# Two expert layers of a hybrid kernel: list constants made early, marks laid out without a step, two result banks, an earlier second list, unread transposes

## What is computed

```
x = x + attn_a(layernorm(x))     # differential attention, 16 heads, causal
x = x + ffn(layernorm(x))        # 8 experts, the best 2 of each token
x = x + attn_b(layernorm(x))     # decayed linear attention, 16 heads of 64
x = x + ffn(layernorm(x))        # the same 8 experts again
```

```
scores = softmax(xf @ router_w.T)              # 2048 tokens x 8 experts
topk_scores, topk_ids = top_k(scores, 2)       # weights, divided by their sum
h   = silu(xf @ w_gate[e]) * (xf @ w_up[e])    # 128 -> 512
out = sum over the two experts of  w * (h @ w_down[e])   # 512 -> 128
```

## Time and profile before

| | us |
|---|---|
| runs of the kernel | 1101.81, 1105.71, 1106.21 (median 1105.71) |
| the profiled execution | 1104.58 |
| its span, first to last instruction | 1102.8 |
| busy in the span: PE, DVE, ACT, POOL | 983.6, 771.8, 733.3, 437.2 |
| mean granted clock of TensorE | 0.962 of 2.4 GHz |

### The profile page before, as it was taken

How to read it: one execution, slowest core, us unless ns; L and a number is a source line. 1 busy time by engine, 2 the same in 40 slices (tenths; PEclk the granted TensorE clock), 3 DMA queues, 4 the chain that set the end, 5 groups by cost and what they waited for, 6 DMA issues and landing times. The chain is left out here.

```text
span 1102.8 us, 27337 instructions
## 1 busy us (share of the span) xinstructions
PE 983.6 (89%) x10398; PEld 663.4 (60%) x10398; DVE 771.8 (70%) x1616; ACT 733.3 (66%) x1475; POOL 437.2 (40%) x584
## 2 busy tenths in 40 slices
PE   5889999999999999964899988999999999489994
PEld 3333333333333333554899877787877887379984
DVE  6789999999999997876433435666766767653342
ACT  4658888888888887624366557677786776445652
POOL 3752212222112221134377433555555553237752
PEclk9889999999999999986999999999999999799998
DMA  2234111111111100241114112121122410011232
GB/s 73 83 95 132 41 31 32 37 54 31 31 31 32 35 27 2 87 144 39 44 54 140 59 49 101 40 78 48 71 100 93 154 69 11 27 42 51 57 87 81
DMA packets 42151, 68.68 MB, mean 62 GB/s; under 512 B 10088, under 2 KB 21096, under 8 KB 40104
## 3 DMA queue, kind: packets, MB, share of 16 engines
q1 hardware_dynamic: 34424, 55.12, 15.5%
q0 software_dynamic: 4992, 10.23, 3.3%
q10 hardware_dynamic: 2608, 1.58, 0.5%
HBM read 51.79 MB, written 14.68 MB: 60 GB/s over the span
## 5 line engine op out<-in xcount | busy, mean ns | idle before, releaser
L803 ACT ACTIVATE PB<-S 128x512 f32<-128x512 f32 x576 | 308.0, 597 | 72.4 <-PE S L609 67.5
L915 DVE TENSOR_REDUCE mx<-S 128x2 f32<-128x1024 f32 (+1 forms) x192 | 207.5, 1127 | 8.6 <-PE S L595 8.6
L871 POOL TENSOR_SCALAR_AFFINE_SELECT PB<-PB 128x512 f32<-128x512 f32 x128 | 79.2, 637 | 307.8 <-ACT PB L803 307.7
L644 PE MATMUL PV<-PB,VP 128*32 128x256 f32 (+2 forms) x2432 | 178.8, 381 | 0.0
L1644 DVE TENSOR_TENSOR m_hs<-m_gs,m_UP 128x512 f32<-128x512 f32 x78 | 53.6, 687 | 141.5 <-ACT m_gs L1530 138.5
L609 PE MATMUL S<-W 50*128 50x512 bf16 (+3 forms) x768 | 124.2, 329 | 4.9 <-ACT PB L803 4.2
L1395 POOL DMA_INDIRECT yd_rows<-m_ys,m_target x78 | 76.8, 985 | 89.0 <-DVE m_ys L1651 77.8
L595 PE MATMUL S<-W 48*128 48x512 bf16 (+3 forms) x640 | 94.5, 326 | 13.1 <-DVE mx L911 4.9
L1526 ACT ACTIVATE m_xt<-m_XT 128x128 f32<-128x128 f32 x78 | 21.6, 277 | 110.7 <-PE m_XT L1437 110.7
L1455 PE MATMUL m_YP<-W,m_hs 128*128 x624 | 84.3, 278 | 11.5 <-DVE m_ys L1651 11.5
L644 PEld LDWEIGHTS PV<-PB,VP 128*32 128x32 f32 x2432 | 51.7, 108 | 69.6 <-issue 59.9
(11 more groups left out here) (384 smaller groups left out, 1892.3 us busy)
## 6 DMA issues: line engine op xcount, KB each, us to landing
d_LQ<-l_rows SPq DMA_DIRECT2D x15, 1024.0 KB, 4.9
W<-qk_parts SPq DMA_DIRECT2D x210, 32.0 KB
qk_parts<-OT SPq DMA_DIRECT2D x24, 256.0 KB, 3.0
W<-qk_parts SPq DMA_DIRECT2D x30, 96.0 KB
W<-in_L_ffn_w_gate SPq DMA_DIRECT2D x1, 2048.0 KB, 9.5
W<-in_L_ffn_w_up SPq DMA_DIRECT2D x1, 2048.0 KB, 14.5
xn_rows<-m_XN SPq DMA_DIRECT2D x8, 256.0 KB, 2.2
m_GA<-yd_rows SPq DMA_DIRECT2D x8, 256.0 KB, 4.3
```

Source lines behind the costliest of these rows:

```text
L644: ins = nc.tensor.matmul(PV[32 * u:32 * u + 32, shift + col:shift + end], VP[:, g, kb, u // 2, :], PB[:, slot, col:end], start=(kb == 0 an ...
L803: nc.scalar.activation(PB[:, j % NPB, :], S2[:, j % 3, :], ACT.Exp, scale=SC).then_inc(exp_done, 1)
L871: nc.gpsimd.affine_select(out=tri, in_=tri, compare_op=ALU.is_ge, fill=0.0, base=0, pattern=[[0, U], [1, P]], channel_multiplier=-1).then_ ...
L915: nc.vector.reduce_max(mx[:, g % 2, c, :, heads[0], qb], S1[:, b, :, 0:w], AX.X)\
```

## The change

1. **Constants.** The constants are allocated once for the whole program (`list_constants`) and made by GpSimd in the attention loop, behind the masks of g == 0 (`make_list_constants`). The semaphore `const_r`, its waits and the memset of `iv` go.
2. **Marks.** `marks` has the tile index i ahead of the planes and slots, so that a product reads its moving operand as one run; VectorE writes (and reads again) the marks through views with the tile index innermost, hence with a step of 3 x slots elements. `place_oh` stays.
3. **Result banks.** `YP` has two banks, used in turn; down(s) waits for y_copy(s-2). The result of the second products moves into the bank of the counts `RC`.
4. **Second list.** `positions` and `late_rows` go ahead of the loop; the marks to slots 0 and 1, the products behind down(2), `other_experts` to slot 2, the sums of the list to the end of slot 3, `make_targets` to 4, `weights` to 5. Three small operations move from `first_bounds` to `second_bounds`. The sums of the list are a copy of the new slots and one addition, in place of three additions.
5. **Unread transposes.** Twenty transposes of the identity stand on TensorE between the first products and the first slot.
6. In `decay_attention` the table `rem` takes the place of `mz`, which is no longer needed by then.

```diff
 def list_products(nc, IV, place_oh, marks, k, start, stop):
-    slots = marks.shape[3]
+    slots = marks.shape[4]
     for i in range(8):
-        last = nc.tensor.matmul(IV[:, 0:planes * slots].rearrange("p (a s) -> p a s", a=planes), place_oh[:, k, :, i],
-                                marks[:, k, 0:planes, :, i], start=(start and i == 0), stop=(stop and i == 7))
+        last = nc.tensor.matmul(IV[:, 0:planes * slots], place_oh[:, k, :, i],
+                                marks[:, k, i, 0:planes].rearrange("p a s -> p (a s)"), start=(start and i == 0),
+                                stop=(stop and i == 7))
...
 def mark_places(nc, chain, tmp, marks, place_oh, slot_no, lane_no, tile_no, iop, k, placed):
-    chain.link(nc.vector.tensor_tensor(marks[:, k, 2], slot_no, ...
-    nc.vector.tensor_tensor(marks[:, k, 0], marks[:, k, 2], ...
-    nc.vector.tensor_scalar(marks[:, k, 1], marks[:, k, 2], ...
+    where, lane, tile = (marks[:, k, :, a].rearrange("p i s -> p s i") for a in (2, 1, 0))
+    chain.link(nc.vector.tensor_tensor(where, slot_no, tmp["slotb"][:, k].unsqueeze(1).to_broadcast(shape), ALU.is_equal))
+    nc.vector.tensor_tensor(tile, where, tile_no.unsqueeze(1).to_broadcast(shape), ALU.mult)
+    nc.vector.tensor_scalar(lane, where, iop, None, ALU.mult)
...
@@ diff_attention, GpSimd, at the end of g == 0
+                            make_list_constants(nc, const)
...
+def make_list_constants(nc, const):
+    nc.gpsimd.memset(const["ones_f"][:], 1.0)
+    nc.gpsimd.memset(const["parts"][:], 0.0)
+    count(const["edges"][:, 0:NT // 2], [[P, NT // 2]], P - 1, 0)
+    count(const["edges"][:, NT // 2:], [[P, NT]], 0, 0)
+    count(const["slot_no"][:], [[1, SLOTS], [0, 8]], 0, 0)
+    count(const["tile_no"][:], [[1, NT]], 1, 0)
+    count(const["iop"][:], [[0, 1]], 0, 1)
+    count(const["lane_no"][:], [[1, P], [0, 8]], 0, 0)
+    count(const["ios"][:], [[1, SLOTS]], 0, 0)
+    count(const["spare"][:], [[P, SLOTS]], 2 * NT * P + 1, 1)
...
@@ moe
-        XT, YP, RC, IV = (ps(k, [P, 512]) for k in ("XT", "YP", "RC", "IV"))
+        XT, RC = (ps(k, [P, 512]) for k in ("XT", "RC"))
+        YP = ps("YP", [P, 2, 512])
...
                 products(IVA, place_a, marks_a, 0)
+                for _ in range(20):
+                    nc.tensor.transpose(GP[:, 1, 0:P], ident[:], ident[:])
                 pe.wait_ge(experts_loaded, loads)
...
                 def down(s, e):
                     pe.wait_ge(h_ready, s + 1)
-                    if s:
-                        pe.wait_ge(y_copied, s)
+                    if s >= 2:
+                        pe.wait_ge(y_copied, s - 1)
...
                     down(s, e)
-                    if s == 3:
+                    if s == 2:
                         products(IVB, place_b, marks_b, 2)
...
                 second_bounds(nc, chain, lists, tmp, RCB)
+                positions(nc, chain, lists, tmp, RCB, lists["rest"][:], lists["whole"][:], OH[:, :, HT:])
+                late_rows()
...
                 for s in range(SLOTS):
                     gate(s)
-                    if s == 0:
-                        positions(nc, chain, lists, tmp, RCB, lists["rest"][:], lists["whole"][:], OH[:, :, HT:])
-                    elif s in (1, 2):
-                        marks_of_second(2 - s)
-                    elif s == 3:
-                        late_rows()
+                    if s in (0, 1):
+                        marks_of_second(1 - s)
+                    elif s == 2:
+                        other_experts(nc, chain, lists, sef, EARLY, etab_ready)
+                    elif s == 4:
+                        make_targets(nc, chain, lists, row, empty, EARLY, SLOTS, targeted)
                     elif s == 5:
-                        other_experts(nc, chain, lists, sef, EARLY, etab_ready)
-                    elif s == 6:
-                        make_targets(nc, chain, lists, row, empty, EARLY, SLOTS, targeted)
-                    elif s == 7:
                         weights()
...
                     if s:
                         y_copy(s - 1)
-                    if s == 4:
+                    if s == 3:
                         other_lists()
...
@@ decay_attention
-        zz, mz, ez, lz, rem = (sb(n, [P, NT, H]) for n in ("zz", "mz", "ez", "lz", "rem"))
+        zz, mz, ez, lz = (sb(n, [P, NT, H]) for n in ("zz", "mz", "ez", "lz"))
+        rem = mz
```

More of the change, by code:

```diff
@@ L1073, in load_experts, with list_constants, count, list_tables @@
                  io["w_down"].rearrange("e (k p) d -> p e k d", p=P)).then_inc(loaded, 16)
-def list_tables(alloc):
+def list_constants(alloc):
     E, NT, SLOTS = Router.E, Router.NT, Router.SLOTS
-    lists = {k: alloc(k, [P, n]) for k, n in (("edges", 3 * NT // 2), ("ones_f", 2 * E + 1), ("parts", 2 * E + 1),
-                                              ("ends", 2 * E + 1), ("full", E), ("rest", E), ("jump", E), ("past", E),
-                                              ("whole", E), ("late", E + 1), ("late_ends", E + 1), ("iop", 1),
-                                              ("spare", SLOTS))}
+    const = {k: alloc("list_" + k, [P, n]) for k, n in (("edges", 3 * NT // 2), ("ones_f", 2 * E + 1), ("parts", 2 * E + 1),
+                                                       ("iop", 1), ("spare", SLOTS))}
+    const["ios"] = alloc("list_ios", [1, SLOTS])
+    for k, shape in (("slot_no", [P, SLOTS, 8]), ("lane_no", [P, P, 8]), ("tile_no", [P, 2, 8])):
+        const[k] = alloc("list_" + k, shape, BF16)
+    return const
+def make_list_constants(nc, const):
+    NT, SLOTS = Router.NT, Router.SLOTS
+    def count(ap, pattern, first, step):
+        nc.gpsimd.iota(ap, pattern, base=first, channel_multiplier=step, allow_small_or_imprecise_dtypes=True)
+    nc.gpsimd.memset(const["ones_f"][:], 1.0)
[8 more added lines that the diff above has]
+    count(const["spare"][:], [[P, SLOTS]], 2 * NT * P + 1, 1)
+def list_tables(alloc, const):
+    E, NT, SLOTS = Router.E, Router.NT, Router.SLOTS
+    lists = dict(const)
+    for k, n in (("ends", 2 * E + 1), ("full", E), ("rest", E), ("jump", E), ("past", E), ("whole", E), ("late", E + 1),
+                 ("late_ends", E + 1)):
+        lists[k] = alloc(k, [P, n])
     lists["counts"] = alloc("counts", [P, 2, E])
-    lists["ios"], lists["sover"] = alloc("ios", [1, SLOTS]), alloc("sover", [1, SLOTS, 3 * E])
+    lists["sover"] = alloc("sover", [1, SLOTS, 3 * E])
     lists["etab"] = alloc("etab", [1, SLOTS], U32)
@@ L1147, in first_bounds @@
     nc.vector.tensor_tensor(parts[:, E + 1:], counts[:, 1], counts[:, 0], ALU.subtract)
-    nc.vector.tensor_scalar(lists["whole"][:], counts[:, 1], float(P), None, ALU.mult)
     chain.link(nc.vector.tensor_scalar(lists["full"][:], counts[:, 0], float(P), None, ALU.mult))
@@ L1162, in second_bounds @@
     over, late, ends = tmp["over"], lists["late"], lists["late_ends"]
+    nc.vector.tensor_scalar(lists["whole"][:], lists["counts"][:, 1], float(P), None, ALU.mult)
+    nc.vector.tensor_tensor(lists["past"][:], lists["rest"][:], lists["counts"][:, 1], ALU.add)
+    nc.vector.tensor_copy(late[:, 0:1], lists["ends"][:, 2 * E:])
     chain.link(nc.vector.tensor_tensor(over[:], n.unsqueeze(2).to_broadcast([P, E, 2 * HT]),
@@ L1368, in _ @@
             def _(pool):
-                def count(ap, pattern, first, step):
-                    nc.gpsimd.iota(ap, pattern, base=first, channel_multiplier=step,
-                                   allow_small_or_imprecise_dtypes=True).then_inc(const_r, 1)
-                nc.gpsimd.memset(lists["ones_f"][:], 1.0).then_inc(const_r, 1)
-                nc.gpsimd.memset(lists["parts"][:, 0:1], 0.0).then_inc(const_r, 1)
-                count(lists["edges"][:, 0:HT], [[P, HT]], P - 1, 0)
-                count(lists["edges"][:, HT:], [[P, NT]], 0, 0)
-                count(slot_no[:], [[1, SLOTS], [0, 8]], 0, 0)
-                count(tile_no[:], [[1, 2 * 8]], 1, 0)
-                count(lists["iop"][:], [[0, 1]], 0, 1)
-                count(lane_no[:], [[1, P], [0, 8]], 0, 0)
-                count(lists["ios"][:], [[1, SLOTS]], 0, 0)
-                count(lists["spare"][:], [[P, SLOTS]], ROWS + 1, 1)
-                nc.gpsimd.memset(iv[:], 0.0).then_inc(const_r, 1)
                 def gather(s):
@@ L1657, in other_lists @@
                     dve.wait_ge(iv_done, 2)
-                    for k in range(3):
-                        last = nc.vector.tensor_tensor(iv[:, k], iv[:, k], IVB[:, k * SLOTS:(k + 1) * SLOTS], ALU.add)
-                    chain.link(last)
+                    more = IVB.rearrange("p (a s) -> p a s", a=3)
+                    nc.vector.tensor_copy(iv[:, :, FIRST:], more[:, :, FIRST:])
+                    chain.link(nc.vector.tensor_tensor(iv[:, :, 0:FIRST], iv[:, :, 0:FIRST], more[:, :, 0:FIRST], ALU.add))
                     make_sources(nc, chain, lists, token, EARLY, SLOTS, sourced)
```

39 lines of the change are left out of this document (15 added, 24 removed).

## The result

The changed kernel takes 1090.51 us (median of four runs, 1088.66 to 1092.49) against 1104.83 for the kernel before: ratio 0.9874, 95% interval 0.9846 to 0.9903. The profiled execution took 1089.87. So it is faster, by 14 us and not by the 25.6 of the forecast, and 1.5 above the top of the range.

What follows compares the result with a forecast made beforehand. Expert layers were taken as bound by TensorE's matmuls, with 15.1 and 13.2 us of loop stalls and VectorE's list chain ahead. Terms summed to -25.6: 1079.0 on the profiled execution, 1080.1 on the median; forecast 1080, range 1073 to 1089.

Steps and rivals of the forecast that it cites:

- marks: Six VectorE operations of the first list's chain, now writing with a step: 0.6 us more, from nothing to 1.5.
- Rival D: VectorE's stepped stores make the kernel slower; gain gone at 4.3 ns more per element, 1113 us at 6.5; chance 0.03.
- Fronts: Each expert layer from first TensorE instruction to first SiLU: forecast 20.5 us in layer 1, 16.1 in layer 2.
- Loops: First to last SiLU per layer: 107.5 and 107.4 us, marks costed at nothing as down() has about 1 us slack.
- Two banks: In the loop, down()'s waits for VectorE's copy of the one result bank, 11.5 us in all, vanish entirely.
- Products: Second list's 16 products inside one slot, 3.04 us before: 1.1 with unstepped columns, between 0.8 and 2.8.
- Rows of slot 8: Slot 8's transposition waits for its gather, 3.0 us late before: 1.4 stays, plus 0.4 for the restart.
- Attention: Moved constants delay a value product behind the first head group's masks: +1.0 us, from 0 to 3.3.
- Layer 2's first up(): Unread transposes raise TensorE's clock there: -1.2 us of 1.6; in layer 1 -0.5 of 1.8.
- A: Second list keeps its price: products stay 2.8 us, clock falls in layer 1, slot 8's gather no earlier; 1088, chance 0.15.
- B: Unread transposes give nothing, the clock being low at the first up() in layer 2 too; 1082 us, chance 0.15.
- C: Banks only rename the wait: down() waits for the gate instead, leaving most of the 11.5 us; 1090, chance 0.05.

Runs made afterwards that it cites:

- the prices above: Flat marks kernel plus 24 unread VectorE operations behind layer 1, timing stepped reads and writes: 1085.39 us in one run with them.
- flat marks: Changed kernel with marks unit-step for VectorE as well as TensorE, slot and tile numbers read with step 0: 1077.21 us, ratio 0.9747.

## Why the prediction was wrong, step by step

**The step that failed: marks.** The mechanism was named, the size was not. I took "the f32 pace", 0.1 us per operation, and called the pace of TensorE's stepped reads, 0.25 per operation, the upper end. Measured: +0.72 for the two tensor_tensor and +0.54 for the tensor_scalar of 184 elements; +1.23 and +0.81 for 312. Both rows I bounded it by were the wrong kind: the f32 row had no step, TensorE's row was a read. In the prices above f32 with a step pays 0.4 ns, a 16-bit store up to 3.9. Rival D, to which I gave 0.03, named the cause and came near the price: its break-even was 4.3 ns an element, measured is 3.5 on the mean of the three operations. Over its 5952 elements that is some 21 us of VectorE (an estimate from the medians); the layers lost only 14, as part of it ran beside other work.

**Where the 14 us of the layers went.** Fronts: +3.1 and +2.2 against the forecast, six operations at 0.5 to 0.7 more, 3.9 in all where I had 0.6; in layer 2 the up() at full clock gave 0.7 of it back. In layer 1 this goes through the late statistics to ScalarE's table loads and weight copy, in layer 2 through the rows of slot 0. Loops: +3.6 and +5.2. I had costed the loop's marks at nothing on a slack of 1 us; the slots overran by 2.1 and 2.3 (4.92 and 5.06 against 2.79), so the gates came late, and in layer 2 the clock fell behind the second wait (interval of 7.27, against 5.79 in layer 1, where it stayed up, and 3.83 with flat marks). That the whole time is off by 10.5 and not by 14 is luck: layer 1 started 3.5 earlier than forecast, through stretches that my sum did not touch.

**What held.** Two banks: m_ys gone from the waits, all summing slots at 2.79. Products 1.14 for 1.1. Rows of slot 8: an interval of 4.10, 1.31 over the slot, and 0.38 for the restart, for 1.4 and 0.4. Parts to scan in 0.36. Attention +1.0: 7.16 to 8.23 between the same two masks. Layer 2's first up() ran at full clock in this profile, worth 1.9 (forecast 1.2). In layer 1 TensorE's clock was 0.50, where I had counted on 0.5 of 1.8 and got nothing: 1.8 was there for 36 more transposes. positions and late_rows fit ahead of the loop; in layer 2 exactly (gate 0 starts at 959.2, right behind late_rows and without a wait). Of the rivals, A did not come; B came in layer 1, and in layer 2 in two other profiles. C's wait for the gate did come, 5.4 of its 11.5, but out of the marks: with flat marks it is 0.1, and the loops keep 2.9 and 2.7 of stall, as forecast.

So the forecast fits the flat kernel, whose marks take the 0.35 and 0.48 us that I had expected of the changed one: 251.0 in the layers against 251.5 (layer 1's first up() 0.5 worse, layer 2's 0.7 better), 1077 against 1080 in all, where most of the 3 lies ahead of layer 1.

## What to carry to other kernels

When a change moves a step from one engine's reads to another's writes, find the price of that very access (type, direction, distance) or measure it in a few unread operations, before a row of another kind is used as its bound. Ask first whether a third loop order has the unit step on both sides; here it cost 0.1 us an operation and gave 13 us. And a cover of 1 us in a slot is a condition with a number: multiply the suspected price by all operations in that slot before costing it at nothing.

## What the runs showed of the hardware

- A 16-bit store of VectorE with a step costs 0.7, 1.7, 3.9 ns an element more at 4, 8, 16 bytes apart (tensor_tensor), and no more at 138 and 234 bytes; a tensor_scalar pays 2.0 at 16 bytes and 2.6 to 3.0 at 138 and 234. A 16-bit tensor_scalar that reads with a step pays 0.6 at 16 bytes; an f32 one in place 0.4 at 32 bytes.
- A 16-bit tensor_tensor that reads one operand with step 0 on the innermost axis takes 0.35 for 0.25 us (184 elements), 0.48 for 0.31 (312).
- TensorE's clock fell to the lower level in the loop behind waits of 2.63 and 2.52 us (list work in the slots of before, 0.51 for 3.4 us) and of 5.28 and 5.73 us (one bank, stepped marks). Behind two late gates of up to 1.2 and 1.7 to 1.8 us it fell in one of four layers: layer 2 of the changed kernel, and not in its layer 1 nor in either layer without the transposes. It did not fall behind waits of 1.00 to 1.14 us for slot 8. And it fell without any wait behind the stepped products of layer 2 (marks of before), so waits alone do not tell when. Where it fell, it cost 1.2 to 1.6 us beyond the wait, and 2.1 to 2.7 with the two longest waits.
- Twenty unread transposes ahead of layer 2's first transposition of rows went with a clock of 1.00 at its first up() in nine profiles of eleven, and the lower level in two; without them it was the lower level in three of three.
- The stage between the layers, the same code in all kernels, took 312.9 to 316.4 us, longest in the two profiles with three separate low stretches of the clock in it. So up to 3 us of a total can come from a stage that the edit does not touch.
